# One graph layer (attention over edges, linear attention, expert layer): destination scores taken by 0/1 products in slot order, edge batches summed one batch later on TensorE

## The reference

```
xn = layernorm(x)
# gnn: softmax over the edges that end in a node, and the node's own loop
h = (xn @ W);  a_src, a_dst = scores of h per node and head (4 heads)
e = leaky_relu(a_src[src] + a_dst[dst], 0.2);  m = segment_max(e, dst)
alpha = exp(e - m[dst]) / segment_sum(...);   gnn = segment_sum(alpha * h[src], dst) + bias
# mix: linear attention with second-order features, 8 heads of 32
q, k normalized;  kv_mod = sum_n k_i k_j v_e;  kv = sum_n k_d v_e
y = 0.5 q_i q_j kv_mod + scale^2 q kv + scale^4 vsum;  mix = (y[1:] / y[0]) @ Wproj.T + bproj
x = x + gnn + mix
# expert layer: 8 experts, the best 2 per token
x = x + sum over the 2 chosen experts of  p * (relu(t @ W1 + b1) @ W2 + b2),  t = layernorm(x)
```

## Time and profile before

| | us |
|---|---|
| median of 3 runs | 2012.85 |
| profiled execution, its own time | 2026.34 |
| its span, first to last instruction | 2024.5 |
| PE busy / VectorE busy / GpSimd busy in the span | 1337.1 / 893.4 / 671.8 |
| mean granted TensorE clock | 0.81 of full speed |

### The profile page before, as it was taken

One profiled execution on the slowest core, in us unless ns is written; L12 is line 12 of the kernel. 1 busy time (PEld: TensorE's weight loads), 2 busy tenths in 40 slices (PEclk: granted clock), 3 DMA queues, 4 the chain that ended last, 5 costly groups with the idle time before them and its releaser, 6 DMA issues.

```text
span 2024.5 us, 25263 instructions
## 1 busy us (share of the span) xinstructions
PE 1337.1 (66%) x7878; PEld 901.2 (45%) x7879; DVE 893.4 (44%) x1722; ACT 378.8 (19%) x1065; POOL 671.8 (33%) x647
## 2 busy tenths in 40 slices
PE   3498335445376676668777777762330999999996
PEld 3354112222133344334343433441320888888885
DVE  6897134333567685434444444441720222232221
ACT  2200000002111111211222221110210333333331
POOL 1300410000022256655666656621436122222222
PEclk8699555666688887888889988875555999999998
DMA  7154311314211112222222222217152122222223
GB/s 236 53 194 142 125 53 52 119 44 127 62 36 38 42 53 79 79 78 73 78 84 81 78 71 79 83 37 275 52 203 81 33 36 33 36 32 35 34 34 84
DMA packets 75645, 164.16 MB, mean 81 GB/s; under 512 B 13845, under 2 KB 50252, under 8 KB 74214
## 3 DMA queue, kind: packets, MB, share of 16 engines
q0 software_dynamic: 32736, 74.39, 14.5%
q1 hardware_dynamic: 41750, 88.13, 12.9%
q10 hardware_dynamic: 1072, 0.53, 0.1%
HBM read 131.82 MB, written 34.36 MB: 82 GB/s over the span
## 4 chain that ended last, share of the span: by engine, by line
PE 45%; issue 15%; DVE 15%; DMA 11%; another core or an unknown queue 5%; POOL 3%; DVEq 2%; SPq 2%; ACT 1%; POOLq 0%; ACTq 0%
PE ps L1157 11%; PE ps L1441 6%; DMA sum_d<-acc 5%; PE ps L1451 5%; PE ps L1173 4%; PE ps L1127 3%; DVE arena L1682 3%; DMA acc<-xs_d 2%; POOL xs_d L838 2%; PE ps L1366 2%; PE ps L1185 2%; PE ps L1241 2%; DVEq L1687 2%; DVE acc L1692 2%
## 5 line engine op out<-in xcount | busy, mean ns | idle before, releaser
L808 POOL DMA_INDIRECT arena<-h_d,tables x440 | 452.8, 1029 | 656.5 <-PE ps L1157 402.2
L1157 PE MATMUL ps<-arena 128*128 128x264 f32 x880 | 282.0, 478 | 172.0 <-DVE acc L1692 127.9
L1157 PEld LDWEIGHTS ps<-arena 128*128 128x128 f32 x880 | 197.4, 235 | 247.1 <-DVE arena L1703 155.1
L1441 PE MATMUL ps<-acc 128*128 128x128 f32 x1792 | 215.4, 279 | 0.1
L1441 PEld LDWEIGHTS ps<-acc 128*128 128x128 f32 x1792 | 207.0, 194 | 3.7 <-ACT acc L1044 0.5
L1451 PE MATMUL ps<-arena,acc 128*128 x896 | 202.5, 379 | 0.0
L999 ACT ACTIVATE arena<-ps 128x1024 f32<-128x1024 f32 (+1 forms) x112 | 99.0, 930 | 493.2 <-PE ps L1354 351.5
L1451 PEld LDWEIGHTS ps<-arena,acc 128*128 128x128 f32 x896 | 166.0, 190 | 20.3
L2027 DVE COPY acc<-arena 128x1024 f32 x112 | 79.6, 712 | 183.9 <-PE ps L1441 146.2
L1185 PE MATMUL ps<-arena 128*32 128x512 f32 (+1 forms) x400 | 83.9, 923 | 104.8 <-DVE arena L1682 103.9
L1053 ACT ACTIVATE acc<-ps,b_s 128x128 f32<-128x128 f32 x448 | 128.2, 369 | 125.3 <-PE ps L1441 125.2
(11 more groups left out here) (343 smaller groups left out, 1543.6 us busy)
## 6 DMA issues: line engine op xcount, KB each, us to landing
arena<-dl_d SPq DMA_DIRECT2D x22, 640.0 KB
arena<-lo_d SPq DMA_DIRECT2D x16, 784.0 KB, 4.5
arena<-in_w SPq DMA_DIRECT2D x4, 2464.0 KB, 17.2
xs_d<-arena SPq DMA_DIRECT2D x1, 7224.0 KB, 27.9
acc<-xs_d SPq DMA_DIRECT2D x56, 129.0 KB, 2.0
arena<-h_d,tables POOLq DMA_INDIRECT x440
arena<-hi_d SPq DMA_DIRECT2D x16, 343.0 KB, 5.0
arena<-in_w SPq DMA_DIRECT2D x4, 1024.0 KB, 13.0
```

Of the source, the lines that this page charges most:

```text
L808: pool.indirect_dma_start(gb[u][:, k, 0:D], None, h_d, bass.IndirectOffsetOnAxis(tsrc[:, j:j + 1], 0)).then_inc(s_gg[u], 16)
L1157: last = MM(ps[:, 6 + s, 0:ACOL], oh[b % 2][:, m, :], gb[u][:, m, :], start=(k == 0), stop=(k == TE - 1))
L1441: last = MM(ps[:, 1 + 2 * (u % 2) + n_, c * P:(c + 1) * P], w1c[n_][:, k, c * P:(c + 1) * P], xfT[u % 2][:, k, :], start=(k == 0), stop=(k ...
```

## The change

1. **Destination scores in slot order.** `d3` goes. In the candidate stage six side pieces are put in, after rounds i = 9, 11, ..., 19: PE turns the destination scores and a 0/1 table of the slots' tiles (`tsel`), multiplies them, and VectorE splits the product in three bf16 parts into `dslot`, 12 columns for each slot. `local_scores` takes its 12 columns from `dslot` at a fixed place, and PE loads no registers for it. The turning of the slot tables (`slot_rows`, `slot_tables`), until now in steps 0 and 1, is the last two side pieces. The side pieces use PSUM bank 5, so the candidates have 5 banks instead of 6. `dslot` lies in the last two gather buffers, so GpSimd gathers 6 batches ahead instead of 8 and goes on once all destination scores are done (`s_dpu`).
2. **Steps.** PE sums the pair features of tile t-4 first and projects then (one step more, 29); `ext` has 3 buffers. VectorE makes the pair features of the two halves apart, before `heads`. Most of `acc` is cleared in step 10.
3. **Edge batches.** PE sums batch b-1 where VectorE prepares batch b; VectorE adds batch b-2 in two halves around the 0/1 matrix, which has 3 buffers. In the mix PE does `use` ahead of the edge batches, and VectorE the edge batches ahead of its terms.
4. **Transfers.** SP loads blocks 0 and 1 of the local destinations ahead of the last score store. The gate weights (`bgb`, `wg_s`, `b1_s`) are loaded after the weights of the mix, not behind the expert weights. `hall` is reloaded by ScalarE's queue.

```diff
+        dslot = view(A, RG0 + (NBUF - 2) * SB * TE * ACOL, NS * 12 // 2).bitcast(BF16).rearrange("p (s h q) -> p s h q", h=GH, q=3)
...
+        SIDE = (9, 11, 13, 15, 17, 19)
...
-        S_T = NT + 3
+        S_T = NT + 4
...
-            store_scores(3)
...
             sp.wait_ge(s_dlst, 32)
             load_locals(0)
+            load_locals(1)
+            store_scores(3)
             sp.wait_ge(s_scd, 16 * 4 * JB)
             sp.dma_start(sco.rearrange("p h e -> p (h e)"), sc_d).then_inc(s_scl, 16)
-            for m in range(1, NL):
+            for m in range(2, NL):
                 load_locals(m)
...
+            sp.dma_start(bgb, rows(bg, P, NE)).then_inc(s_gw, 16)
+            sp.dma_start(wg_s, wg).then_inc(s_gw, 16)
+            sp.dma_start(b1_s[:, :], b1).then_inc(s_w2, 16)
...
             sp.wait_ge(s_accd, NS)
-            for c in range(LC):
-                sp.dma_start(hall[:, c * LW:(c + 1) * LW, :],
-                             h_d.rearrange("(t p) c -> p t c", p=P)[:, c * LW:(c + 1) * LW, 0:D]).then_inc(s_x[c], 16)
             sp.dma_start(A[:, RG0:BO], w12[:, RG0:BO]).then_inc(s_w1, 16)
-            sp.dma_start(bgb, rows(bg, P, NE)).then_inc(s_gw, 16)
-            sp.dma_start(wg_s, wg).then_inc(s_gw, 16)
-            sp.dma_start(b1_s[:, :], b1).then_inc(s_w2, 16)
...
-            pool.wait_ge(s_slc, 2)
+            pool.wait_ge(s_sided, 6)
...
-            for b in range(NBUF, NBT):
+            pool.wait_ge(s_dpu, NL)
+            for b in range(NBUF - 2, NBT):
...
+            act.wait_ge(s_accd, NS)
+            for c in range(LC):
+                act.dma_start(hall[:, c * LW:(c + 1) * LW, :],
+                              h_d.rearrange("(t p) c -> p t c", p=P)[:, c * LW:(c + 1) * LW, 0:D]).then_inc(s_x[c], 16)
...
+            def side(k):
+
+                if k:
+                    pe.wait_ge(s_sided, k)
+                if k == 0:
+                    for h in range(GH):
+                        last = TR(ps[0:NT, 5, h * P:(h + 1) * P], nas[:, :, GH + h], identf[:, :])
+                if k == 1:
+                    for u in range(2):
+                        last = TR(ps[0:NT, 5, u * P:(u + 1) * P], tsel[:, u, :], identf[:, :])
+                if k in (2, 3):
+                    for h in range(2):
+                        hh = 2 * (k - 2) + h
+                        last = MM(ps[:, 5, h * NS:(h + 1) * NS], adT[0:NT, hh * P:(hh + 1) * P], tselT[0:NT, 0:NS],
+                                  start=True, stop=True)
+                if k in (4, 5):
+                    pe.wait_ge(s_slf, 1)
+                    for m in range(2 * TE):
+                        j = m % TE
+                        last = TR(ps[:, 5, m * P:(m + 1) * P], (fsrc, fdl)[m // TE][:, k - 4, j * P:(j + 1) * P], identf[:, :])
+                last.then_inc(s_side, 1)
             for i in range(NQ + 1):
                 if i < NQ:
                     candidates(i)
                 if i:
                     collect(i - 1)
+                if i in SIDE:
+                    side(SIDE.index(i))
             pe.wait_ge(s_w, 16 * 6)
             pe.wait_ge(s_fm, P)
+            pe.wait_ge(s_sided, 6)
...
                 for b in edges(step):
-                    aggregate(b)
+                    if b:
+                        aggregate(b - 1)
...
                 for s in range(LS):
-                    t = pe.value_load(ts_row[0:1, m * LS + s:m * LS + s + 1], min_val=0, max_val=NT - 1)
                     for k in range(TE):
                         j = s * TE + k
                         c = (m % 2 * LS * TE + j) * 12
-                        last = MM(ps[:, 5, c:c + 12], dlb[m % 2][:, j * P:(j + 1) * P], d3[:, ds(t * 12, 12)],
+                        last = MM(ps[:, 5, c:c + 12], dlb[m % 2][:, j * P:(j + 1) * P],
+                                  dslot[:, m * LS + s, :, :].rearrange("p h q -> p (h q)"),
                                   start=True, stop=True)
                 last.then_inc(s_dpu, 1)
...
                 t = step
+                if t >= 4:
+                    sums(t - 4)
                 if t < NT:
                     project(t)
-                if step == 0:
-                    slot_rows()
-                if t >= 3:
-                    sums(t - 3)
                 edge_sums(step)
-                if 0 <= t - 2 < NT:
-                    q_T(t - 2)
                 if step < S_BULK:
                     for m in (2 * step, 2 * step + 1):
                         local_scores(m)
+                if 0 <= t - 2 < NT:
+                    q_T(t - 2)
...
                 if n < ZR:
                     pair_sums(n)
+                if n:
+                    use(n - 1)
+                if n < ZR:
                     (gram_products, half_shifts, denominators, spread)[c](r)
                 edge_sums(S_A + n)
-                if n:
-                    use(n - 1)
...
+            aggregate(NBT - 1)
...
-            st(V.tensor_copy(part[2], r0))
-            d3v = d3[:, :].rearrange("p (t h q) -> p t h q", h=GH, q=3)
...
-            V.tensor_copy(d3v[:, :, :, 2], r1).then_inc(s_prep, 1)
+            for u in range(2):
+                V.tensor_scalar(tsel[:, u, :], iota_f[:, 0:NT], ts_p[:, u:u + 1], None, ALU.is_equal)
+            V.tensor_copy(part[2], r0).then_inc(s_prep, 1)
...
+            def side(k):
+                dve.wait_ge(s_side, k + 1)
+                if k == 0:
+                    V.tensor_copy(adT[0:NT, :], ps[0:NT, 5, :]).then_inc(s_sided, 1)
...
+                    v = ps[:, 5, 0:2 * NS].rearrange("p (h s) -> p h s", h=2)
+                    q = [dslot[:, :, 2 * (k - 2):2 * (k - 1), s].rearrange("p s h -> p h s") for s in range(3)]
+                    st(V.tensor_copy(q[0], v))
+                    V.tensor_tensor(dres, v, q[0], ALU.subtract).then_inc(s_sided, 1)
+                    dve.wait_ge(s_sided, k + 1)
+                    st(V.tensor_copy(q[1], dres))
+                    st(V.tensor_tensor(dres, dres, q[1], ALU.subtract))
+                    st(V.tensor_copy(q[2], dres))
+                if k in (4, 5):
+                    u = k - 4
+                    n = min(P, NS - u * P)
+                    v = ps[:, 5, :].rearrange("p (w k s) -> p w k s", w=2, k=TE)
+                    o, e = u * P * TE, (u * P + n) * TE
+                    V.tensor_copy(tsrc[:, o:e].rearrange("p (s k) -> p k s", k=TE), v[:, 0, :, 0:n])
+                    V.tensor_copy(tdl[:, o:e].rearrange("p (s k) -> p k s", k=TE), v[:, 1, :, 0:n]).then_inc(s_sided, 1)
...
+                if n % JB == 2 and n // JB - 1 in SIDE:
+                    side(SIDE.index(n // JB - 1))
...
+            def pairs(t, g):
...
+                if t:
+                    dve.wait_ge(s_kv, KD * (t - 1) + g + 1)
...
+            def accumulate(b, s):
...
+                q = acc[:, ds(t * ACOL, ACOL)]
+                V.tensor_tensor(q, q, ps[:, 6 + s, 0:ACOL], ALU.add).then_inc(s_accd, 1)
...
                 for b in edges(step):
                     u = b % NBUF
                     m = b * SB * TE
                     if b >= 2:
-                        dve.wait_ge(s_agg, SB * (b - 1))
-                    V.tensor_tensor(oh[b % 2], under(iota_f[:, :], SB * TE), over(tdl[:, m:m + SB * TE], P), ALU.is_equal)
+                        accumulate(b - 2, 0)
+                    if b >= OB:
+                        dve.wait_ge(s_agg, SB * (b - OB + 1))
+                    V.tensor_tensor(oh[b % OB], under(iota_f[:, :], SB * TE), over(tdl[:, m:m + SB * TE], P), ALU.is_equal)
+                    if b >= 2:
+                        accumulate(b - 2, 1)
                     dve.wait_ge(s_gg[u], 16 * SB * TE * (b // NBUF + 1))
                     v = gb[u][:, :, 0:D].rearrange("p k (h c) -> p k h c", c=GD)
                     V.tensor_tensor(v, v, over(wm[:, m:m + SB * TE, 0:GH], GD), ALU.mult).then_inc(s_msg, 1)
-                    if b:
-                        accumulate(b - 1)
...
-                V.memset(C, 0.0).then_inc(s_accz, 1)
+                V.memset(flag, 0.0).then_inc(s_accz, 1)
...
                 t = step
                 if 0 <= t - 2 < NT:
                     done = norms_a(t - 2)
+                    done = norms_b(t - 2, done)
+                    unit(t - 2, done)
+                if 0 <= t - 3 < NT:
+                    pairs(t - 3, 0)
                 if 0 <= t - 1 < NT:
                     summed = squares_a(t - 1)
-                if 0 <= t - 2 < NT:
-                    done = norms_b(t - 2, done)
-                if 0 <= t - 1 < NT:
                     squares_b(t - 1, summed)
-                if 0 <= t - 2 < NT:
-                    unit(t - 2, done)
+                if 0 <= t - 3 < NT:
+                    pairs(t - 3, 1)
                 if t < NT:
                     heads(t)
-                if t >= 3:
-                    pairs(t - 3)
-                if step == 1:
-                    slot_tables()
...
+                if step == S_BULK - 1:
```

(13 more changed lines are left out.)

148 lines of the change are left out of this document (67 added, 81 removed).

## The result

The changed kernel took 1789.35 us (median of 4 runs, 1785.0 to 1791.6), beside 2014.34 us for the kernel before on the same chip: ratio 0.888, 95% interval 0.886 to 0.890. The forecast was 1733 us, between 1680 and 1820. The time lies in the range, 56 us above the forecast and above the 1690 to 1775 that the forecast case gave itself. The profiled execution has a span of 1789.9 us against 2024.5, so 234.6 us are to be found. That is more than the 225 us between the medians, because the profiled execution before lay 13.5 us above its median and this one only 2.3.

A forecast was written before the change was run, and what follows sets the result against it. Limits were seen stage by stage: PE, register-load issue, a serial ring, PE and GpSimd floors in the mix, full DMA engines. Terms +4-41-103-4-32-2-90+3-15 = -280 gave span 1744.5, execution 1746, median 1733 us, range 1680 to 1820.

The forecast's parts named there:

- Bulk steps: Steps 2 to 10: PE's register-load issue goes (99 us by itself), 155 us instead of 258, -103 us (-118 to -68).
- Rival 2: Loads of local destinations hold steps 2 to 10 at 19 us a step; kernel 1767 us; chance 0.08.
- Steps 0 and 1: Register loads and slot-table turning leave these steps, half of VectorE's 17 us stall stays: -41 us (-54 to -19).
- Prelude and candidates: Stage before step 0: PE's added small products and VectorE's 16 added operations cost, +4 us (-3 to +10).
- I take 2 us off: Candidates: gain from dropping the `d3` instructions, one of which stood 13.7 us beside GpSimd's big addition; only one round won.
- Steps 12 to 24: Sums use the step before's pair features, cutting the serial ring: 11.0 us a step instead of 13.7, -32 us (-38 to -15).
- Mix: PE's 154.6 us wait for messages goes; GpSimd's 435 us floor plus 52 and 11: 498 instead of 588, -90 us.
- Rival 1: VectorE's work holds GpSimd's gathers in the mix: kernel 1816 us, or 1775 with half of it; chance 0.17.
- Rival 3: Both floors reached: mix 445, bulk 141, reload gains 30; kernel 1651 us, or 1680 with stalls left; chance 0.08.
- Rival 4: PE's clock at its lower level from candidates to mix makes the kernel slower, 2156 us; chance 0.02.
- Rival 5: The edge batches' lag fails because VectorE's additions come late; mix stays at 588, kernel 1823 us; chance 0.05.
- Reload: Between mix and experts: early gate weights and h's changed load order start VectorE's first product sooner, -15 us (-30 to -5).

The follow-up runs named there:

- e_regs: The changed kernel with the register load put back on PE ahead of each slot's two local-score products (220 loads, value unused): 1904.65 us, ratio 0.946.
- e_side: The changed kernel with VectorE's four remaining operations on the slot-order scores issued one by one between candidate products, not in one block: 1662.79 us, ratio 0.853.
- e_exp: The changed kernel with ScalarE's exponential of the final maxima ahead of its five loads of h, on a chip without the stalls: 1666.71 us, ratio 0.854.
- e_lag0: The changed kernel with the edge batches' lag undone: PE sums batch b right after its messages, VectorE adds batch b-1: 1857.03 us, ratio 0.921.
- e_pause3: The changed kernel with GpSimd waiting, ahead of every third batch, until the gathers of the batch before have landed: 1779.67 us, ratio 0.882.
- after_again: The changed kernel itself, no edit, run again on the chip of the last group of runs: 1782.82 us, ratio 0.884.

## Why the prediction held, and where its steps failed

The forecast was 45 us too low on the span, and the other 11 of the 56 are the gap of profile and median. The time lies inside the range by luck in part, because errors of both signs met: the bulk steps, step 11, the end of the mix and the experts gave 37 us more than I had said, the six other terms 83 less.

- *Bulk steps: right mechanism, size 23 us short.* The 99 us of issue measured 96 (228.9 - 132.9 in e_regs). The other edits gave 29.5 more (258.4 to 228.9), where I had added time for loads of local destinations and uncovered scans. That was the failed step: the loads do hold the chain of the steps 2 to 10 for 8.7%, some 11 us, and PE waits 28.6 us for 0/1 columns, but the rest of the stage shrank by more. Which edit did that, the earlier pair features or another, was not tried. Rival 2 (19 us a step) is out at 14.7. Step 11 came within 1 us. Steps 0 and 1 came within 3, but by luck: of the 17 us that VectorE had stood behind a finished projection I let half stay, and 17.1 stayed.
- *Prelude and candidates: failed, +16.5 instead of +4.* PE did start 13.7 us earlier, but the stage from its first product to step 0's projection grew from 99.0 to 129.2 us. Of these 30 us, 10.1 are PE's wait for GpSimd's addition, now inside the stage; with it "I take 2 us off" comes out about right, 3.6. The failed step is the price of VectorE's added work, "about 8.6 us at 0.4 to 0.7 us" an operation in two blocks "of some 3 us", +3. The 16 operations took 15.2 us, the blocks 6.2 each, against a slack of 11:

```profile
L1652 DVE CAST arena<-ps 128x440 bf16<-128x440 f32 x2 | 4.2, 2112 | 0.0
L1655 DVE CAST arena<-arena 128x440 bf16<-128x440 f32 x2 | 2.3, 1136 | 0.1
```

  The blocks held PE 5.2 and 3.5 us. Behind the first wait the granted clock stood at its lower level (0.50, 1.2 GHz), and a batch's 12 products took 4.16 us instead of 2.19; behind the second 3.15. With its own side products and the lower clock PE's busy time in the stage grew by 11.4 us. But e_side, which took both waits and the clock's part away, got only 4 us back: as far as it shows, the amount of VectorE's work counted more than where it stood.
- *Steps 12 to 24: -12.5 instead of -32.* The ring is cut as said, but PE's batch now waits for VectorE's addition of the batch before, which comes after the heads of the same step: 40.6 us. The granted clock is lower than before (0.79 against 0.84), the feature sums come late, and VectorE waits 36.5 us for them; that the one follows from the other is read from the traces, not tried. At a granted clock of 0.79 a step takes 12.7 us; on the chip of e_exp, at 0.93, 10.2. My 11.0 lies between. The tail, with one step more, cost 7.7.
- *Mix: -67 instead of -90, right limit, floor and stalls mis-sized.* GpSimd's chain does set it: 357 + 94 + 33.5 + 19.5 = 504 of 520 us, and 451 where there are no stalls, against my floor of 435. Two terms of the 498 failed. The floor was 16 us too low: a gather was busy 1.066 us instead of 1.028 (13 us), and its issue took 94.2 instead of 90.4. And "none of the edits touches them" was wrong of the unknown-queue pieces, which I kept at 52 us: they grew to 142, while GpSimd's waits for PE fell from 116.8 to 19.5 us. Where such pauses were given back the pieces shrank, to 70 us in e_lag0 and 49 in e_pause3. By what stands in the chain they are far more than they cost: above the floor of 451 us the mix has 69 us, where I had 52 + 11 = 63, and with 49 us of pieces in e_pause3 it took 513 instead of 520. PE's idle time before the batches' products, 83.5 us, also missed the sign I gave (under 50).
- *Rival 1* (VectorE holds the gathers) has little: a mean of 1.066 us against 1.028 before, 13 us for 335 gathers.
- *Rival 3* (both floors reached) came true in the bulk steps alone: 132.5 us against its 141; the mix took 520 against its 445, the reload won nothing.
- *Rival 4* (slower through the clock) did not come in the mix (0.88 against 0.87), but in small, in the candidates and steps 12 to 24, it is what two of the terms lost.
- *Rival 5* falls with e_lag0: the lag works, and gives most outside the mix.
- *Reload: 0 instead of -15.* Failed step: "only the order can win", with h's order as the gain. The order lost. ScalarE's queue takes the five loads in 28.7 us, holds ScalarE, whose exponential VectorE needs (28.2 us of wait), and h lands 3 to 4 us later than from SP's queue. VectorE's first product started at 1185.1 us, not before 1159 as my sign had it. What seems to have gained is the gate weights' early load, some 8 us, which I had only counted as clearing the way. The Trainium skill, DMA: Bandwidth & Descriptors, Issuing engines are not separate DMA queues, says that another issuing engine saves only the time of issue. The traces agree that another queue won nothing: 28.5 us on ScalarE's against 24.8 on SP's.

## What to carry to other kernels

Before removing an engine's waits, ask what else those pauses let through: here, with GpSimd's gathers running without gaps, PE's signals to three engines came up to 21 us late. When work is moved to another engine's queue, count what that engine has to do behind it, and compare chips before adding runs of different groups. Price an added operation by a row of its own shape, not by the nearest row: 0.4 to 0.7 us was said, 2.1 was measured. A long GpSimd instruction is priced by the one VectorE instruction that it holds; cut it, don't move it.

## What the runs showed of the hardware

- With gathers every 1.25 us, ScalarE, VectorE and GpSimd started up to 21.4 us after the PE product that they waited for had ended. Each started within 0.3 us of PE's semaphore update, which was recorded that late; some went on when the DMA engines had run dry, others, the end of the longest piece among them, in the middle of the stream. In one of four groups of runs, with the same gathers, there was none of this. The whole kernel before is 67 us faster there (1946.8 against 2014.2), e_exp 116 us faster than after_again.
- What delays PE's updates stays open. Late loading of instructions does not show as the cause: the instruction queues' packets are few (46 and 37 in the span), and from 658 to 677 us, at the end of the stalls shown above, the DMA queues carried nothing but the gathers:

```profile
q0 software_dynamic: 635, 1.71, 31.3%
```

- Pauses in the stream shorten the stalls (19.8 to 6.4 us in the mix), and cost GpSimd about what they give back in a stage that it bounds.
- A register load on PE, its value unused, costs 0.44 to 0.46 us of issue between short products and was not hidden behind them; 220 of them cost 122 us in all.
- A 4 by 127 operation took 14.01 us beside one long GpSimd instruction, and a 3136-column one 1.03 us beside 25 short ones.
